# Moving the loads of the next head's keys, queries and values from the first unit of a head to behind its first two projection tasks

## The chip, the core and the metric

The kernel runs on one core of a Trainium2 chip. The metric is the device time of one execution in microseconds (us). TensorE (PE), VectorE (DVE), ScalarE (ACT), GpSimd (POOL) and SyncE (SP) each run their own list of instructions and meet through semaphores. SP computes nothing here: it issues transfers, one after the other, to 16 DMA engines that all queues share.

## The reference, cut to what matters

Two transformer-like layers follow one another. The part that this text is about is the first attention: 1024 latent tokens and 6404 context rows of width 128 are normalised, and 16 heads of width 64 are computed over 7428 keys (context and latents).

```python
q = lat @ Wq
kv = jnp.concatenate([x, lat], axis=1) @ Wkv
k, v = jnp.split(kv, 2, axis=-1)
dots = jnp.einsum('bhid,bhjd->bhij', q, k) * scale     # 16 heads, 1024 x 7428
attn = jax.nn.softmax(dots, axis=-1)
out = jnp.einsum('bhij,bhjd->bhid', attn, v)
```

After it come an output projection, a layer of experts, a second attention and a second layer of experts.

## The kernel before, in words

`stage_attention` works head by head. A head has 60 units (`UNITS`), numbered g = 0 to 59; a unit takes two tiles of 128 keys against half of the queries. In each unit PE makes scores (L583, L584), ACT takes the exponential (L725), POOL splits off the low half of the probabilities (L518) and PE multiplies high and low halves by the values (L599, L601, L611). Beside this, PE scores for the running maximum of the next head from unit 24 on (`OFFSET`, L559) with a reduction on DVE (L788).

Heads go in pairs: head b = 2i (the even head, e = 0) and head 2i + 1 (the odd head, e = 1). During a pair, every third unit has a task that projects a block for the next pair: in the even head 17 tasks for queries and keys, in the odd head 15 tasks for values. A task is a chain: PE projects into bank Y (L531 to L533 or L541 to L543), ACT copies the high half into a staging buffer (`copy_kq`, L689, or `copy_v`, L697), DVE writes the low half (L765, L773), SP writes both to device memory (L419 and L420, or L428). There are two staging buffers of each kind (`NR` = 2), so task n uses buffer n % 2, and ACT waits with the copy of task n until the write of task n - 2 has landed (semaphores `kq_out`, `v_out`). That wait stands in ACT's one list, in front of the exponentials of the units that follow.

At the start of head b, SP loads what head b + 1 needs into the other half of the double buffers: `load_kq` (six transfers, 3.2 MB: keys twice, low keys, queries) and, in an even head, also `load_v` (1.9 MB). The wait ahead of it is for the last score of head b - 1. The values of the next even head are loaded in unit 51 of the odd one.

PE, ACT and DVE run the pairs in a hardware loop of seven turns (`Fori(0, HEADS // 2 - 1)`), whose body is two heads; the last pair is straight code behind it. So there are six backward jumps, each at the start of an even head (b = 2, 4, ... 12). POOL has a loop of its own over one head. SP's list has no loop.

Of the kernel before, what the change touches and what calls it, by code (L numbers as in the profile page):

```python
# [26 lines left out]
HEADS, DH = 16, 64  # L27
# [286 lines left out]
def stage_attention(nc, pers, A):  # L314
# [5 lines left out]
    with sc:  # L320
# [48 lines left out]
        TASKS = KQ_TASKS + V_TASKS  # L369
        TASK_STEP = 3  # L370
        BACK_AT, FRONT_AT = 26, 56
        EARLY = 2 * (UNITS - OFFSET)
        FIRST_SLOTS = [[]] * 3 + [list(range(n, n + EARLY // 12)) for n in range(0, EARLY, EARLY // 12)]

# [6 lines left out]
        def task_at(e, g):  # L381

            n = g // TASK_STEP
            if g % TASK_STEP or n >= (V_TASKS if e else KQ_TASKS):
                return None
            return KQ_TASKS + n if e else n
# [19 lines left out]
        def _(sp):  # L406
# [3 lines left out]
            def write_kq(i, n, high, low, done):  # L410

                sp.wait_ge(y_split, i * TASKS + n + 1)
                r, w = slice(i * P, (i + 1) * P), twidth(n)
                if n < Q_TASKS:
                    oh, ol = (d[r, n * BANK:n * BANK + w] for d in (q_high, q_low))
                else:
                    c = (n - Q_TASKS) * BANK
                    oh, ol = (d[r, c:c + w] for d in (k_high, k_low))
                sp.dma_start(oh, high[:, 0:w]).then_inc(done, 16)  # L419
                sp.dma_start(ol, low[:, 0:w]).then_inc(done, 16)  # L420

            def write_v(i, n):
                sp.wait_ge(y_split, i * TASKS + n + 1)
                r, tt = (n - KQ_TASKS) % NR, vtiles(n)
                w = full_tiles(n)
                c = slice(tt[0] * VCOLS, (tt[0] + w) * VCOLS)
                o = v_all[2 * i * P:(2 * i + 2) * P, c].rearrange("(a p) c -> p a c", p=P)
                sp.dma_start(o, stage_v[r][:, :, 0:w, :].rearrange("p a t c -> p a (t c)")).then_inc(v_out[r], 16)  # L428
                if w < len(tt):
                    c = slice(FULL_TILES * VCOLS, KEY_TILES * VCOLS)  # L430
                    for a in range(2):
                        o = v_all[(2 * i + a) * P:(2 * i + a) * P + TAIL, c]
                        sp.dma_start(o, stage_v[r][0:TAIL, a, w, :]).then_inc(v_out[r], 16)

            def v_writes(i, r):

                tasks = [n for n in range(KQ_TASKS, TASKS) if (n - KQ_TASKS) % NR == r]
                return OUT0 + 16 * i * sum(1 if full_tiles(n) == len(vtiles(n)) else 3 for n in tasks)

            def kq_writes(i, r):  # L440
                return OUT0 + 32 * (i - 1) * len(range(r, KQ_TASKS, NR))

            def load_kq(m):
                e = m % 2
                sp.dma_start(kc[0:DH, e, :], k_high[rows(m), :]).then_inc(k_in[e], 16)
                sp.dma_start(kc[DH:P, e, :], k_high[rows(m), :]).then_inc(k_in[e], 16)
                sp.dma_start(qc[0:DH, e, :], q_high[rows(m), :]).then_inc(q_in[e], 16)
                sp.dma_start(qc[DH:P, e, :], q_low[rows(m), :]).then_inc(q_in[e], 16)
                sp.dma_start(qd[0:DH, e, :], q_high[rows(m), :]).then_inc(q_in[e], 16)
                sp.dma_start(kd[0:DH, e, :], k_low[rows(m), :]).then_inc(k_in[e], 16)  # L450

            def load_v(m):
                e, whole = m % 2, FULL_TILES * VCOLS
                sp.dma_start(v[:, e, 0:FULL_TILES, :].rearrange("p t c -> p (t c)"),
                             v_all[m * P:(m + 1) * P, 0:whole]).then_inc(v_in[e], 16)
                sp.dma_start(v[0:TAIL, e, FULL_TILES, :], v_all[m * P:m * P + TAIL, whole:KEY_TILES * VCOLS])\
                  .then_inc(v_in[e], 16)
# [12 lines left out]
            for b in range(HEADS):  # L470
                i, e = divmod(b, 2)
                projecting = i + 1 < HEADS // 2
                for g in range(UNITS):
                    if g == 0 and b + 1 < HEADS:
                        if b:
                            sp.wait_ge(scored, b * UNITS)
                        if b and e:
                            for r in range(NR):
                                sp.wait_ge(kq_out[r], kq_writes(i + 2, r))
                        load_kq(b + 1)  # L480
                        if not e:
                            if b:
                                sp.wait_ge(low_done, LOW0 + b * UNITS)
                            load_v(b + 1)
                    if projecting:
                        n = task_at(e, g)
                        if n is not None and n < KQ_TASKS:
                            r = n % NR
                            write_kq(i + 1, n, stage_h[r], stage_l[r], kq_out[r])
                        elif n is not None:  # L490
                            write_v(i + 1, n)
                        if e and g == LAST - 8:
                            for r in range(NR):
                                sp.wait_ge(v_out[r], v_writes(i + 2, r))
                            sp.wait_ge(low_done, LOW0 + b * UNITS)
                            load_v(b + 1)
# [264 lines left out]
        def _(dve):  # L761
# [43 lines left out]
            def head(b, e, with_max, projecting, i):  # L805
                for g in range(UNITS):
                    m, _, n = slots_at(b, e, g)
                    slots = with_max or m is b
                    if slots:
                        take(m, n)  # L810
                    t = task_at(e, g - 1) if projecting and g else None
                    if t is not None:
                        split_task(i + 1, t)
                    if slots:
                        take(m, n + 1)
                        if n + 2 in (SLOTS // 2, SLOTS):
                            finish_max(m, 0 if n + 2 < SLOTS else 1)
                    if g % SIDE == PAIRS:
                        normalize_half(b, g // SIDE)
# [734 lines left out]
def build(nc, a, out):  # L1554
    attention = dict(x=a["x"], ctx=a["ctx_1024"], ln_m_g=a["L0_xattn_ln_m_g"], ln_m_b=a["L0_xattn_ln_m_b"],
                     ln_l_g=a["L0_xattn_ln_l_g"], ln_l_b=a["L0_xattn_ln_l_b"], wq=a["L0_xattn_Wq"],
                     wkv=a["L0_xattn_Wkv"], wout=a["L0_xattn_Wout"])
    experts0 = dict(control=a["L0_ffn_controller"], up=a["L0_ffn_f1"], up_bias=a["L0_ffn_bias"], down=a["L0_ffn_f2"])
    cross = dict(ctx=a["ctx_1024"], w_cq=a["L1_xattn_w_cq"], b_cq=a["L1_xattn_b_cq"], w_c=a["L1_xattn_w_c"],
                 b_c=a["L1_xattn_b_c"], w_q=a["L1_xattn_w_q"], b_q=a["L1_xattn_b_q"], w_l=a["L1_xattn_W_l"],  # L1560
                 b_l=a["L1_xattn_b_l"])
    experts1 = dict(control=a["L1_ffn_Wc"], control_bias=a["L1_ffn_bc"], up=a["L1_ffn_W1"], up_bias=a["L1_ffn_b1"],
                    down=a["L1_ffn_W2"], down_bias=a["L1_ffn_b2"])
    whole = Scope(nc, "all")
    with whole:
        pers = Persistent(whole)
        shared = Scope(nc, "shared")
        with shared:
            for_attention(pers, shared)
            stage_prepare(nc, pers, attention)  # L1570
            stage_attention(nc, pers, attention)
            stage_attention_out(nc, pers, attention)
        whole.clear_semaphores()
        later = Scope(nc, "later", whole)
        with later:
            for_later_stages(pers, later)
            ahead = dict(ctx=cross["ctx"], up=experts1["up"], down=experts1["down"])
            stage_experts(nc, pers, experts0, "experts0", 0, ahead=ahead)
            stage_cross(nc, pers, cross)
            stage_experts(nc, pers, experts1, "experts1", 1, out)  # L1580
# [26 lines left out]
```

## Time and profile before

| what | value |
| --- | --- |
| median of three runs | 2737.18 us (2736.98 to 2744.89) |
| time of the profiled execution | 2738.75 us |
| its span, first to last instruction | 2737.0 us |
| PE busy / ACT / DVE / POOL | 92% / 49% / 62% / 67% |
| mean granted TensorE clock | 0.963 of full speed |
| data moved by the DMA engines | 172.13 MB |

The span is what the trace covers; the profiled execution's time is 1.75 us more than its span and 1.57 us above the median. Busy times are unions of an engine's instructions. A time at the start of a row of a timeline is in us from the span's start; in square brackets at its end stands how long the engine sat idle before it, and what released it. "issue" there means that no semaphore of the profile explains the wait. The granted clock of 1.00 is TensorE's upper level (2.4 GHz), 0.50 the lower (1.2 GHz).

### The profile page before, as it was taken

How to read it: one execution, taken by the hardware profiler on the slowest of the kernel's cores; microseconds unless marked ns; L12 is line 12 of the kernel's file. 1: busy time of each engine (PE TensorE's matmuls, PEld its weight loads, DVE VectorE, ACT ScalarE, POOL GpSimd, SP SyncE). 2: the span in 40 equal slices, each digit the busy share in tenths (PEclk: the TensorE clock that was granted, in tenths of full speed). 3: DMA queues.
4: the chain of work that ended last, by engine and by line, in shares of the span. 5: the costliest groups of instructions: out<-in, count | busy, mean ns of one | idle time of the engine just before them, and what ended most of it. 6: DMA issues, size and time to landing. Idle time of an engine off the chain costs nothing. (4 is left out here: it accounts for less than half of the span.)

```text
span 2737.0 us, 83713 instructions
## 1 busy us (share of the span) xinstructions
PE 2515.7 (92%) x33785; PEld 1679.6 (61%) x33785; DVE 1693.1 (62%) x3186; ACT 1343.9 (49%) x1627; POOL 1840.3 (67%) x1056
## 2 busy tenths in 40 slices
PE   3479998999899989998999899989999999769996
PEld 1236665666566656665666566656666666547884
DVE  8566665666566656665666566656666662248764
ACT  4125554555455545554555455545555555227652
POOL 1128887888788878887888778877888999501001
PEclk9779999999999999999999999999999999879998
DMA  2441314131413141213122321232132200150000
GB/s 83 142 137 40 75 41 120 40 75 42 119 43 76 41 119 41 67 48 100 60 59 60 91 69 52 64 83 77 39 80 69 56 2 2 59 127 1 2 2 11
DMA packets 98555, 172.13 MB, mean 63 GB/s; under 512 B 10280, under 2 KB 87664, under 8 KB 92656
## 3 DMA queue, kind: packets, MB, share of 16 engines
q1 hardware_dynamic: 94864, 162.46, 20.7%
q8 instruction: 285, 4.67, 0.8%
q10 hardware_dynamic: 3296, 4.10, 0.5%
q14 instruction: 110, 0.90, 0.1%
HBM read 100.72 MB, written 65.81 MB: 61 GB/s over the span
## 5 line engine op out<-in xcount | busy, mean ns | idle before, releaser
L518 POOL TENSOR_TENSOR att_prob_low<-att_prob 128x1024 f16<-128x1024 f32 x960 | 1787.8, 1864 | 488.4 <-ACT att_prob L725 407.0
L788 DVE TENSOR_REDUCE att_part<-all_banks 128x1 f32<-128x512 f32 (+1 forms) x1920 | 1242.1, 669 | 753.6 <-PE all_banks L559 736.9
L725 ACT ACTIVATE att_prob<-all_banks 128x1024 f32<-128x1024 f32 x960 | 968.8, 1009 | 874.4 <-PE all_banks L584 805.7
L559 PE MATMUL all_banks<-att_kc,att_qc 128*128 128x512 f16 (+1 forms) x1920 | 718.9, 379 | 96.0 <-issue 72.9
L583 PE MATMUL all_banks<-att_qc,att_kc 128*128 128x512 f16 (+1 forms) x1888 | 719.5, 381 | 0.7 <-issue 0.7
L584 PE MATMUL all_banks<-att_qd,att_kd 128*128 128x512 f16 (+1 forms) x1888 | 719.6, 381 | 0.0
L599 PEld LDWEIGHTS all_banks<-att_v,att_prob 128*128 128x128 bf16 x7552 | 537.9, 99 | 131.7 <-issue 15.5
L599 PE MATMUL all_banks<-att_v,att_prob 128*128 128x65 f16 x7552 | 594.3, 193 | 5.8 <-ACT att_prob L725 5.8
L601 PE MATMUL all_banks<-att_v,att_prob 128*128 128x64 f16 x7552 | 595.9, 194 | 0.5 <-issue 0.5
L601 PEld LDWEIGHTS all_banks<-att_v,att_prob 128*128 128x128 bf16 x7552 | 505.6, 97 | 100.3 <-issue 0.3
L611 PEld LDWEIGHTS all_banks<-att_v,att_prob_low 128*128 128x128 f16 x7552 | 351.0, 97 | 115.7 <-POOL att_prob_low L518 6.4
L611 PE MATMUL all_banks<-att_v,att_prob_low 128*128 128x65 f16 x7552 | 382.1, 193 | 5.8 <-POOL att_prob_low L518 2.9
L584 PEld LDWEIGHTS all_banks<-att_qd,att_kd 128*128 128x128 f16 (+1 forms) x1888 | 184.6, 98 | 211.9 <-issue 4.4
L559 PEld LDWEIGHTS all_banks<-att_kc,att_qc 128*128 128x128 f16 x1920 | 186.1, 98 | 141.6 <-issue 81.1
L583 PEld LDWEIGHTS all_banks<-att_qc,att_kc 128*128 128x128 f16 (+1 forms) x1888 | 184.7, 98 | 135.7 <-issue 10.5
L982 POOL MEMSET experts_tie<- 128x1 f32 x64 | 2.2, 98 | 225.4 <-POOLq L1177 195.6
L697 ACT ACTIVATE att_stage_v<-all_banks 128x512 f16<-128x512 f32 (+1 forms) x120 | 70.8, 591 | 148.5 <-PE all_banks L543 122.1
L689 ACT ACTIVATE att_stage_h<-all_banks 128x512 f16<-128x512 f32 (+1 forms) x119 | 69.6, 585 | 81.5 <-PE all_banks L533 74.0
L773 DVE TENSOR_TENSOR att_stage_v<-all_banks,att_stage_v 128x256 f16<-128x256 f32 (+1 forms) x240 | 87.2, 405 | 34.4 <-ACT att_stage_v L697 33.5
L1359 DVE TENSOR_TENSOR cross_pt_l<-all_banks,cross_pt_h 128x512 f16<-128x512 f32 (+1 forms) x112 | 70.8, 641 | 36.2 <-ACT cross_pt_h L1309 35.8
L541 PE MATMUL all_banks<-shared_wv_h,shared_kvh 128*128 (+2 forms) x472 | 89.3, 225 | 1.0 <-DVE att_prob L765 1.0
L543 PE MATMUL all_banks<-shared_wv_h,shared_kvl 128*128 (+2 forms) x472 | 89.6, 225 | 0.0
(272 smaller groups left out, 2066.3 us busy)
## 6 DMA issues: line engine op xcount, KB each, us to landing
att_v<-v_all SPq DMA_DIRECT2D x16, 1870.5 KB
att_kc<-k_high SPq DMA_DIRECT2D x32, 928.5 KB, 10.9
v_all<-att_stage_v SPq DMA_DIRECT2D x112, 258.0 KB, 2.5
att_kd<-k_low SPq DMA_DIRECT2D x16, 928.5 KB, 15.3
k_high<-att_stage_h SPq DMA_DIRECT2D x98, 128.0 KB, 1.7
k_low<-att_stage_l SPq DMA_DIRECT2D x98, 128.0 KB, 1.9
prep_ctx<-in_ctx SPq DMA_DIRECT2D x5, 640.0 KB, 10.4
later_ctx<-in_ctx SPq DMA_DIRECT2D x1, 3200.0 KB
```

The lines of the kernel that those rows point to most:

```text
L518: pool.tensor_tensor(prob_low[g % NL][0:n, 0:w], p[:, 0:w], p.bitcast(BF16)[:, 1:2 * w:2], op=ALU.subtract).then_inc(low_split, 1)
L541: pe.matmul(o, th, wh, start=True, stop=False)
L543: last = pe.matmul(o, tl, wh, start=False, stop=True)
L559: pe.matmul(X[n % 2][:, 0:kwidth(c)], qc[:, e, j * P:(j + 1) * P], kc[:, e, c * BANK:c * BANK + kwidth(c)], start=True, stop=True).then_in ...
L583: pe.matmul(o, kc[:, e, t * P:t * P + n], qc[:, e, q], start=True, stop=False)
L584: last = pe.matmul(o, kd[:, e, t * P:t * P + n], qd[:, e, q], start=False, stop=True)
L599: pe.matmul(O[:, o:o + DH + 1], w, v[:, e, t, 0:DH + 1], start=False, stop=False, skip_group_check=True)
L601: last = pe.matmul(O[:, o:o + DH], w, v[:, e, t, DH + 1:VCOLS], start=False, stop=False, skip_group_check=True)
L611: last = pe.matmul(O[:, o:o + DH + 1], w, v[:, e, t, 0:DH + 1], start=False, stop=True, skip_group_check=True)
L725: act.activation(o, i, ACT.Exp, scale=SCALE).then_inc(exp_done, 1)
L773: last = dve.tensor_tensor(st[:, a, 0:w, DH + 1:VCOLS], y, st[:, a, 0:w, 0:DH], op=ALU.subtract)
L788: dve.tensor_reduce(part[:, j, c:c + 1], X[n % 2][:, 0:kwidth(c)], axis=AX.X, op=ALU.max)\
```

## The change

The condition under which SP issues the loads in `block.sync` goes from unit 0 to unit 4. SP's list is written unit by unit, and tasks 0 and 1 of a head stand at units 0 and 3, so the loads now stand behind the writes of these two tasks and before the write of task 2.

```diff
         BACK_AT, FRONT_AT = 26, 56
+        LOAD_AT = 4
...
                 for g in range(UNITS):
-                    if g == 0 and b + 1 < HEADS:
+                    if g == LOAD_AT and b + 1 < HEADS:
                         if b:
                             sp.wait_ge(scored, b * UNITS)
                         if b and e:
                             for r in range(NR):
                                 sp.wait_ge(kq_out[r], kq_writes(i + 2, r))
                         load_kq(b + 1)
                         if not e:
                             if b:
                                 sp.wait_ge(low_done, LOW0 + b * UNITS)
                             load_v(b + 1)
```

SP's list at the start of an even head, before. The names h0, l0, h1 and l1 are the two staging buffers of high and low halves; kc, kd, qc, qd and v are the loaded operands:

```order
L445 DMA att_kc<-k_high 64x7428
L446 DMA att_kc<-k_high 64x7428
L447 DMA att_qc<-q_high 64x1024
L448 DMA att_qc<-q_low 64x1024
L449 DMA att_qd<-q_high 64x1024
L450 DMA att_kd<-k_low 64x7428
L454 DMA att_v<-v_all 128x7482
L456 DMA att_v<-v_all 4x129
L419 DMA q_high<-att_stage_h0 128x512
L420 DMA q_low<-att_stage_l0 128x512
L419 DMA q_high<-att_stage_h1 128x512
L420 DMA q_low<-att_stage_l1 128x512
```

The same place on SP with the change (all line numbers are one higher), from the write of task 1 on:

```order
L420 DMA q_high<-att_stage_h1 128x512
L421 DMA q_low<-att_stage_l1 128x512
L446 DMA att_kc<-k_high 64x7428
L447 DMA att_kc<-k_high 64x7428
L448 DMA att_qc<-q_high 64x1024
L449 DMA att_qc<-q_low 64x1024
L450 DMA att_qd<-q_high 64x1024
L451 DMA att_kd<-k_low 64x7428
L455 DMA att_v<-v_all 128x7482
L457 DMA att_v<-v_all 4x129
L420 DMA k_high<-att_stage_h0 128x512
L421 DMA k_low<-att_stage_l0 128x512
```

The eight loads have moved from ahead of the write of task 0 to between the writes of tasks 1 and 2. In an odd head SP's list before is the loads and then the writes of values:

```order
L449 DMA att_qd<-q_high 64x1024
L450 DMA att_kd<-k_low 64x7428
L428 DMA v_all<-att_stage_v0 128x2x516
L428 DMA v_all<-att_stage_v1 128x2x516
L428 DMA v_all<-att_stage_v0 128x2x516
```

and with the change:

```order
L429 DMA v_all<-att_stage_v1 128x2x516
L446 DMA att_kc<-k_high 64x7428
L447 DMA att_kc<-k_high 64x7428
L448 DMA att_qc<-q_high 64x1024
L449 DMA att_qc<-q_low 64x1024
L450 DMA att_qd<-q_high 64x1024
L451 DMA att_kd<-k_low 64x7428
L429 DMA v_all<-att_stage_v0 128x2x516
```

Here six loads have moved behind two writes. In head 14 no tasks stand in the list, and its loads stay where they were. The lists of PE, ACT, DVE and POOL are the same before and after.

## Rows read from the trace of the kernel before

**Rows 1.** Who waited for whom: us in total, times, longest

```profile
PE all_banks L559 <- issue: 72.9, 7, 22.1
```

**Rows 2.** Windows, an even and an odd head: busy us, instructions, clock, DMA

```profile
448.50:592.80 144.30, 135.36 (x1845) 85.76 (x1845) 88.26 (x144) 71.68 (x79) 111.87 (x61) 0.96 0.24 68
592.80:725.60 132.80, 132.79 (x1971) 90.03 (x1972) 87.93 (x158) 70.75 (x79) 111.84 (x61) 1.00 0.25 70
```

**Rows 3.** Timeline of PE at the first jump, and at the sixth

```profile
452.28 0.53 PE L611 MATMUL all_banks<-att_v,att_prob_low 128*128 128x65 f16 x12
461.75 0.61 PE L559 MATMUL all_banks<-att_kc,att_qc 128*128 128x512 f16 x1 [8.94 <-issue]
...
1848.68 0.61 PE L559 MATMUL all_banks<-att_kc,att_qc 128*128 128x512 f16 x1 [8.92 <-issue]
```

**Rows 4.** DMA queues: packets, MB, share; 451.3:457.7, then 457.7:459.5

```profile
q1 hardware_dynamic: 107, 1.35, 101.7%
...
q8 instruction: 1, 0.02, 4.7%
q14 instruction: 2, 0.02, 4.5%
```

**Rows 5.** Instruction packets: 306.0:307.0, 314.4:315.4, none until 328.8:329.8

```profile
q8 instruction: 1, 0.02, 6.2%
...
q8 instruction: 1, 0.02, 6.0%
...
q8 instruction: 1, 0.02, 8.6%
```

**Rows 6.** Windows at the first jump, behind the sixth, and behind 201.28

```profile
452.80:455.10 2.30, 0.01 (x1) 0.00 (x0) 0.61 (x2) 0.00 (x0) 1.03 (x1) 0.99 1.00 213
...
461.75:465.30 3.55, 3.55 (x9) 1.41 (x10) 1.38 (x2) 0.60 (x1) 1.45 (x1) 0.50 0.97 203
...
1848.68:1854.53 5.85, 5.85 (x43) 3.38 (x44) 1.38 (x2) 1.62 (x2) 2.08 (x2) 0.50 0.99 237
201.28:205.89 4.61, 4.61 (x47) 3.17 (x48) 1.44 (x3) 1.59 (x2) 3.79 (x2) 0.50 0.16 57
```

**Rows 7.** Timeline of SP, ACT and PE in head 0

```profile
182.80 0.43 SPq L420 DMA_DIRECT2D q_low<-att_stage_l  x1
...
199.72 0.60 ACT L689 ACTIVATE att_stage_h<-all_banks 128x512 f16<-128x512 f32 x1 [7.46 <-DMA q_low<-att_stage_l]
...
201.28 0.24 PE L599 MATMUL all_banks<-att_v,att_prob 128*128 128x65 f16 x1 [5.37 <-ACT att_prob L725]
```

**Rows 8.** Timeline of SP in head 2: loads, second write, third write

```profile
448.54 0.45 SPq L445 DMA_DIRECT2D att_kc<-k_high  x1
...
474.68 0.32 SPq L419 DMA_DIRECT2D q_high<-att_stage_h  x1
475.05 0.43 SPq L420 DMA_DIRECT2D q_low<-att_stage_l  x1
481.44 0.32 SPq L419 DMA_DIRECT2D k_high<-att_stage_h  x1
```

**Rows 9.** Timeline of ACT in head 2, copy of task 4

```profile
491.73 0.60 ACT L689 ACTIVATE att_stage_h<-all_banks 128x512 f16<-128x512 f32 x1 [0.58 <-PE all_banks L533]
```

**Rows 10.** DMA issues, us to landing: from 467.9, from 330.3

```profile
q_low<-att_stage_l SPq DMA_DIRECT2D x1, 128.0 KB, 5.5
...
v_all<-att_stage_v SPq DMA_DIRECT2D x1, 258.0 KB, 4.0
```

**Rows 11.** Timeline of head 1: SP's loads and writes, ACT's fifth copy

```profile
315.00 0.45 SPq L445 DMA_DIRECT2D att_kc<-k_high  x1
...
323.61 28.13 SPq L428 DMA_DIRECT2D v_all<-att_stage_v  x5
...
348.36 0.61 ACT L697 ACTIVATE att_stage_v<-all_banks 128x512 f16<-128x512 f32 x1 [0.76 <-PE all_banks L543]
```

**Rows 12.** Timeline of PE in head 1

```profile
331.76 0.20 PE L611 MATMUL all_banks<-att_v,att_prob_low 128*128 128x65 f16 x1 [0.53 <-issue]
```

## The prediction, made before the changed kernel had run

> **What bounds the kernel now.** I read the windows of whole heads first. An odd head keeps PE busy for 132.79 of 132.80 us; an even head behind a jump takes 144.30 us with PE busy for 135.36 [rows 2]. So PE bounds both, every us in which PE stands adds to the time, and even heads have some 9 us of standing that odd ones lack. The list of waits names it: PE waited seven times before L559 for nothing that a semaphore explains, 72.9 us in all, the longest 22.1 us [rows 1]. That longest one lies ahead of the first head, at 104 us. The other six are (72.9 - 22.1) / 6 = 8.47 us each, and the timeline puts them at the six backward jumps: 8.94 us at the first, 8.92 at the last [rows 3]. PE had ended at 452.81 (452.28 + 0.53) and went on at 461.75.
>
> What PE waits for is its own code. After SP issued the loads from 448.54 on, no packet of an instruction queue (q8, q14) is seen from 451.3 to 457.7, while the load's queue q1 alone fills the DMA engines (101.7%); then q8 and two of q14 come together, and work goes on behind them [rows 4]. That the loads make code late also shows where nothing jumps. In running code q8 brings a packet about every 8.3 us (one in 306.0:307.0, one in 314.4:315.4), but under the loads of head 1 the next comes only in 328.8:329.8, about 14.3 us after the last, 6.0 us late [rows 5], and PE starves for 0.53 us [rows 12].
>
> The stop has a second price. Behind it TensorE runs at a granted clock of 0.50 (1.2 GHz), having stood idle before: 3.55 us behind the first jump, 5.85 behind the sixth [rows 6], on average 4.46 over the six. At half speed that loses half of it, 2.2 us. A jump so costs 8.47 + 2.2 = 10.7 us.
>
> **Part 1: the jump without the loads.** The changed SP list puts the loads behind the write of task 1, some 13 us after PE goes on, so the jump's code meets empty DMA queues. The trace has no such jump. Lower bound of the gain: the code is no less than 4.9 us late, since PE stopped at 452.81 and no code packet came before 457.7 [rows 3, 4], and if a shorter stop still lowers the clock nothing else is gained: about 5.0 us per jump. Upper bound: code comes 6.3 us earlier and the clock stays up, 8.5 us. I take 5.8 us, a little under the 6.0 of running code [rows 5], which leaves PE idle for about 2.7 us, and I take it that such a stop leaves the clock at its upper level, since after PE's end at 452.81 the records still show 0.99 until 455.1 [rows 6]. That is 5.8 + 2.2 = 8.0 us per jump, **-48 us** over six.
>
> **Part 2: even heads, a write behind the loads.** The moved item is eight transfers in a queue that serves in order. What is late next is the write of task 2, which is now issued behind them and which frees staging buffer 0 for the copy of task 4. Before, it was the write of task 0 that stood behind the loads, and the jump's standstill hid that.
>
> Head 0 has no jump and shows the stall undisguised. The low write issued at 182.80, behind the loads, held ACT's copy until 199.72, idle 7.46 us; PE then stood for 5.37 us [rows 7]. A copy that nothing holds follows an idle time of 0.58 us [rows 9]. So the copy was 7.46 - 0.58 = 6.9 us late, and PE has a slack of 6.9 - 5.37 = 1.5 us. Behind it the clock was low for 4.61 us [rows 6], 2.3 us lost: 7.7 us in all.
>
> Now the same for a head with the change, by the distances of head 2. The write of task 1 ends its issue at 475.05 + 0.43, about 475.5 [rows 8]: call this L, the moment of the first load. The write of task 2 is issued at 481.44, L + 6 [rows 8]. The copy of task 4 starts at 491.73, L + 16.2 [rows 9]. When does the write land? Before, the low write issued at 468.30 took 5.5 us, so it landed at 473.8, 25.3 us after the first load at 448.54 [rows 8, 10]; a free write of this size takes about 2 us, so the queue of loads held it. I take 25 us. The copy is 25 - 16.2 = 8.8 us late, PE stands 8.8 - 1.5 = 7.3 us, and with 2.3 us of low clock the head pays 9.6 us. Ends: 7.6 if the write lands after 23 us because PE's stop is gone, 10.4 at 25.3 us with a longer low clock. Six heads: **+58 us**. Head 0 already pays 7.7, so it adds **+1.9 us**.
>
> **Part 3: odd heads.** The loads are six transfers here. SP issues them at 315.00 [rows 11]; the write of values from 330.3 on landed 4.0 us later, at 334.4 [rows 10], 19.4 after the first load. With the change the first load stands behind that write, at 330.8. The write of the third task is then behind the loads and lands at 330.8 + 19.4 = 350.2. The fifth copy starts at 348.36 [rows 11]: 1.8 us late, 1.5 of it in the slack, 0.3 us on PE. Seven heads: **+2.4 us**, between 0 and 7.
>
> **What costs nothing.** The loads land later, but the first reader is the maximum of unit 24, and they end some 25 us after unit 5, near unit 17; the values are read in the next head. SP's wait in front of the loads is for a score long past. In head 14 nothing moves. Code packets in the shifted loads come late while PE runs: one starvation like [rows 12] in each of 14 heads would be 7 us, but some heads had it already; I take 0 and keep 5 for the range.
>
> **The sum.** 2738.75 (the profiled execution, 1.57 us over the median) - 48 + 58 + 1.9 + 2.4 = 2753 us; less 1.57 this is 2751 us against the median. A big gain and a big loss all but cancel. The turning point: with the jump at -8.0, the change pays only if the stall of an even head is under about 7.3 us.
>
> **Rivals.**
> - *The code is late for another reason, and the jump stays as it is.* Then part 1 is 0: 2737 + 58 + 1.9 + 2.4 = 2799 us. For it: a taken jump needs new code whatever else runs, and no jump here is seen without loads. Against it: the packet that is 6.0 us late in head 1, where nothing jumps [rows 5]. The Trainium skill speaks for this rival ("DMA: Bandwidth & Descriptors", section on queues, rings and completion order): a DMA engine takes turns between the queues it has work for, packet by packet, so that a code packet would wait for little more than one packet of the loads. By that rule the loads could not make the jump long and the time would be the 2799 us above; by the row it is 2751. The trace disagrees with the rule so far.
> - *Writes are not held by the loads* (the faster side). If the write of task 2, issued only 6 us behind the first load, slips through by L + 17.7, the stall of even heads is gone: 2737 - 48 - 7.7 (head 0's too) + 0 = 2682 us; half of it gone leaves about 2715. It decides at L + 23: later than that the change loses. Against it: head 0's writes, issued at 182.80, did not land before 199 [rows 7].
> - *Even balance.* The loads end a little sooner (23.3 us), the stall costs 7.9 us, and all of it comes to within 8 us of 2737.
>
> **How the numbers follow.** What a measurement here can tell from no change is about 0.3%, 8.2 us. Main case with a stall of 8 to 10.4 us: 0.60; even balance: 0.20; jump stays: 0.09; writes slip through or stall under 7 us: 0.11. Slower by over 0.3%: 0.60 and 0.09, less some of the main case's low end: 0.66. Within: 0.22. Faster: 0.12. The main case's own range: -51 to -30 from part 1, +45 to +62 from even heads, 0 to +12 from the rest, that is 2731 to 2781. The 80% range leaves out most of the two far cases: 2729 to 2783.
>
> **What the profile will show.** Right: PE's idle before L559 at the six jumps is 2 to 4 us instead of 8.5; the low clock behind jumps is gone; and in seven even heads ACT's L689 waits some 9 us for a write of k_low, PE some 7 us for L725, about 30 us into the head, with low clock behind. Wrong if the jumps still cost 8 us (first rival), if L689 waits for no DMA (second), or if PE stands at the jump for under 1 us. Odd heads should be within 1 us of 133.

## The result, and the profile after

The changed kernel takes 2761.01 us (median of 6 runs, 2758.62 to 2763.37) against 2737.14 us before. The medians lie 23.9 us apart; the ratio estimated from all runs is 1.0078, with a 95% interval from 1.0067 to 1.0090, which is 21 us (18 to 25). The changed kernel is slower. The prediction had 2751 us, in 2729 to 2783, and slower as the likeliest case. The span of the profiled execution is 2756.8 us, 19.8 more than before.

First the waits of the changed kernel that answer to [rows 1] and [rows 7] (us in total, times, longest):

```profile
ACT att_stage_h L690 <- DMA k_low<-att_stage_l: 62.3, 7, 9.2
PE all_banks L600 <- ACT att_prob L726: 59.2, 16, 7.1
ACT att_stage_v L698 <- DMA v_all<-att_stage_v: 53.0, 8, 23.3
PE all_banks L560 <- issue: 35.8, 7, 21.8
```

The last row is the one in which the jumps stand. Without the one long wait ahead of head 0, (35.8 - 21.8) / 6 = 2.33 us are left per jump, where it was 8.47. The first row is new: in seven even heads ACT's copy waits for a write of low keys. The second is what that does to PE: 59.2 us of standing in front of L600, of which before there were 5.4 us in head 0 and crumbs. The third row holds a wait of 23.3 us before the loop, as before, and seven new ones of 3.7 to 5.1 us in odd heads.

The timeline of PE in head 2, at the jump and at the new stop, against [rows 3]:

```profile
455.50 0.39 PE L560 MATMUL all_banks<-att_kc,att_qc 128*128 128x512 f16 x1 [2.10 <-issue]
...
493.67 0.23 PE L600 MATMUL all_banks<-att_v,att_prob 128*128 128x65 f16 x1 [6.83 <-ACT att_prob L726]
```

and SP and ACT between the two, against [rows 8] and [rows 9]:

```profile
466.72 0.32 SPq L420 DMA_DIRECT2D q_high<-att_stage_h  x1
467.08 0.43 SPq L421 DMA_DIRECT2D q_low<-att_stage_l  x1
467.56 0.47 SPq L446 DMA_DIRECT2D att_kc<-k_high  x1
...
473.84 0.43 SPq L421 DMA_DIRECT2D k_low<-att_stage_l  x1
...
492.10 0.60 ACT L690 ACTIVATE att_stage_h<-all_banks 128x512 f16<-128x512 f32 x1 [8.91 <-DMA k_low<-att_stage_l]
```

The loads start at 467.56. The low write of task 2 is issued at 473.84, 6.3 us behind them, and the copy that waits for it starts at 492.10, 24.5 us behind the first load. Its idle time of 8.91 less the usual 0.58 is 8.3 us of lateness; PE stands for 6.83.

The windows (same columns as [rows 2]) show what each head pays, and where the clock is low:

```profile
452.00:596.90 144.90, 135.97 (x1842) 86.40 (x1841) 88.38 (x144) 71.52 (x80) 111.97 (x60) 0.98 0.24 68
596.90:732.20 135.30, 133.07 (x1968) 89.92 (x1967) 88.05 (x158) 70.56 (x79) 111.83 (x60) 1.00 0.24 69
455.50:459.00 3.50, 3.50 (x45) 2.25 (x46) 1.39 (x3) 1.62 (x2) 2.08 (x2) 1.00 0.03 7
737.40:740.80 3.40, 3.40 (x39) 2.45 (x38) 0.99 (x2) 1.34 (x2) 0.97 (x2) 0.50 0.01 2
493.70:498.40 4.70, 4.70 (x46) 3.05 (x47) 1.71 (x3) 1.47 (x2) 3.78 (x2) 0.50 0.18 61
```

The even head is as long as before (144.9 against 144.3 us): it stands for 144.90 - 135.97 = 8.93 us, now 2.10 at the jump and 6.83 at the late copy. The odd head (head 3) takes 135.3 us and stands for 2.23 us, where it stood for 0.01; I had said within 1 us of 133. Behind the first jump the clock stays at 1.00. Behind the second it is at 0.50 for 3.4 us, and behind the late copy for 4.7 us.

### The profile page after: what moved, and what is told of

Read it like the earlier page. It is cut to its first block and busy times, and to the rows that moved or that the text cites. A ratio compares the mean times of both kernels' runs of the same rounds, so it can differ in the third digit from the quotient of the medians.

```text
span 2756.8 us, 83713 instructions
## 1 busy us (share of the span) xinstructions
PE 2519.1 (91%) x33785; PEld 1680.3 (61%) x33785; DVE 1694.9 (61%) x3186; ACT 1342.1 (49%) x1627; POOL 1841.5 (67%) x1056
## 5 line engine op out<-in xcount | busy, mean ns | idle before, releaser
L560 PE MATMUL all_banks<-att_kc,att_qc 128*128 128x512 f16 (+1 forms) x1920 | 720.3, 379 | 58.7 <-issue 35.8
L600 PEld LDWEIGHTS all_banks<-att_v,att_prob 128*128 128x128 bf16 x7552 | 540.2, 99 | 190.0 <-ACT att_prob L726 73.7
L600 PE MATMUL all_banks<-att_v,att_prob 128*128 128x65 f16 x7552 | 597.6, 193 | 59.3 <-ACT att_prob L726 59.2
L766 DVE TENSOR_TENSOR att_stage_l<-all_banks,att_stage_h 128x512 f16<-128x512 f32 (+1 forms) x119 | 79.3, 666 | 45.3 <-ACT att_stage_h L690 45.3
L1360 DVE TENSOR_TENSOR cross_pt_l<-all_banks,cross_pt_h 128x512 f16<-128x512 f32 (+1 forms) x112 | 70.9, 642 | 36.3 <-ACT cross_pt_h L1310 35.8
```

The source lines that it names most:

```text
L560: pe.matmul(X[n % 2][:, 0:kwidth(c)], qc[:, e, j * P:(j + 1) * P], kc[:, e, c * BANK:c * BANK + kwidth(c)], start=True, stop=True).then_in ...
L600: pe.matmul(O[:, o:o + DH + 1], w, v[:, e, t, 0:DH + 1], start=False, stop=False, skip_group_check=True)
L766: dve.tensor_tensor(low[:, 0:w], src[:, 0:w], high[:, 0:w], op=ALU.subtract).then_inc(y_split, 1)
```

## The experiments

Each ratio is against the kernel before, run beside it on the same chip. The kernel before had medians from 2738.93 to 2739.65 us there.

**Even heads alone, and odd heads alone.** The two runs split the change.

```diff
-                    if g == LOAD_AT and b + 1 < HEADS:
+                    if g == (0 if e else LOAD_AT) and b + 1 < HEADS:     # e1; e2: (LOAD_AT if e else 0)
```

> The loads move behind tasks 0 and 1 in even heads alone; in odd heads they stay at unit 0. My theory (jump freed, one write held behind the loads): PE idle at the six jumps about 2.3 us, ACT's L689-copy of task 4 idle some 9 us in seven even heads, no copy of values waits for a DMA. The even heads of the changed kernel were 8.4 us longer in sum than before, head 0 0.3 shorter, so about +8 us: 2745. Rival (the odd heads' loss comes from the even heads' change, by loads that drain later or code that comes late): the odd heads stay long by 14 us, and the time is near 2760.

> The loads move in odd heads alone; in even heads they stay at unit 0, so the jumps stay at 8.5 us idle. My theory: the seven odd heads lose what they lost in the changed kernel, 14 us, all of it by the copy of the fifth values task waiting for the write behind the loads: 2751. Rival (odd heads lose because the even head before them changed): no change, 2737.

Measured: e1 2753.2 us, ratio 1.0047 (1.0035 to 1.0059), and e2 2749.53 us, ratio 1.0041 (1.0027 to 1.0054). The two excesses add up to 0.88%, the change itself has 0.78%. The waits of e1:

```profile
ACT att_stage_h L690 <- DMA k_low<-att_stage_l: 63.1, 7, 10.0
PE all_banks L560 <- issue: 35.5, 7, 21.5
ACT att_stage_v L698 <- DMA v_all<-att_stage_v: 24.7, 4, 22.9
```

and of e2:

```profile
PE all_banks L560 <- issue: 71.8, 7, 21.5
ACT att_stage_v L698 <- DMA v_all<-att_stage_v: 51.3, 8, 23.1
ACT att_stage_h L690 <- DMA q_low<-att_stage_l: 8.5, 1, 8.5
```

In e1 the short jumps and the seven late copies of keys come together, and of the odd heads' waits for values 1.8 us in three are left (24.7 - 22.9). In e2 the jumps are long again ((71.8 - 21.5) / 6 = 8.4 us), and the seven waits for values are there. Each loss belongs to its own kind of head, so the rival of both runs falls. e1 came out 14 us above the kernel before, 6 more than I had expected from the even heads of the changed kernel. In its trace the clock accounts for that. It was low behind all six short jumps, as here behind the first (columns as in [rows 2]):

```profile
456.72:459.89 3.17, 3.17 (x8) 1.25 (x9) 1.38 (x2) 0.60 (x1) 1.59 (x1) 0.50 0.03 8
```

The changed kernel had it low behind two of the six. That is 13 us more at the lower level, 6.5 us lost.

**A third staging buffer.** If the write held behind the loads is the cause, a buffer that is needed one task later takes it away and leaves the loads where they are.

```diff
-        NR = 2
+        NR = 3
...
-            sp.wait_ge(filled, 4)
+            sp.wait_ge(filled, NR + 2)
```

> The changed kernel with three staging buffers of each kind instead of two, so that a copy waits for the write three tasks back. The held copy of an even head comes 6.75 us later, which takes its lateness from about 8.3 to 1.6 us, within the slack of 1.5 to 2 us; in odd heads it is gone. My theory: jumps 2.3 us idle with the clock up (-48 to -52 us), head 0's old stall gone (-8), no new stall: 2678 to 2690. Rival (the stops in even heads come from the loads themselves, beside running PE, and not from the wait for the write): the stops of 7 us stay and the time is near 2750.

Measured: 2689.92 us, ratio 0.9819 (0.9795 to 0.9842), 49 us faster than before and some 70 us faster than the change with two buffers. Its waits:

```profile
PE all_banks L560 <- issue: 35.6, 7, 21.9
ACT att_stage_h L690 <- DMA k_low<-att_stage_l: 15.3, 7, 2.6
PE all_banks L600 <- ACT att_prob L726: 2.0, 6, 0.7
```

The copies still wait, but 2.2 us each (15.3 / 7), 1.6 late, and of 59.2 us of standing on PE 2.0 are left. The loads run beside PE exactly as in the changed kernel, so they are not what stopped it.

**The control: a third buffer without the change.** The same edit on the kernel before.

> Control for the third staging buffer: the kernel before, loads at unit 0, with three buffers of each kind. My theory: only head 0's stop (5.4 us and 2.3 us of low clock) goes, the jumps stay at 8.5 us: about 2730. Rival (the third buffer alone is what gained the 49 us): 2690.

Measured: 2730.95 us, ratio 0.9963 (0.9949 to 0.9977).

```profile
PE all_banks L559 <- issue: 74.1, 7, 21.7
ACT att_stage_h L689 <- DMA q_low<-att_stage_l: 1.7, 1, 1.7
```

The jumps stay at (74.1 - 21.7) / 6 = 8.7 us, and only head 0's stop goes. The buffer alone gives 9 us. The other 40 us of e3 come from moving the loads, once nothing waits behind them.

**Half the dose.** The changed kernel, but the values of an even head are loaded from unit 28.

```diff
+        LOAD_AT, LOAD_V_AT = 4, 28
...
                         load_kq(b + 1)
-                        if not e:
-                            if b:
-                                sp.wait_ge(low_done, LOW0 + b * UNITS)
-                            load_v(b + 1)
+                    if g == LOAD_V_AT and not e:
+                        if b:
+                            sp.wait_ge(low_done, LOW0 + b * UNITS)
+                        load_v(b + 1)
```

> The changed kernel, two buffers, with one thing less behind task 1 of an even head: the values are loaded from unit 28, keys and queries stay at unit 4. The write of task 2 then stands behind six transfers instead of eight. My theory: it lands some 20 us after the first load instead of 25, the copy of task 4 is 3 to 4 us late as in odd heads (3.0 to 4.4), PE stands 1 to 2.5 us instead of 7 in seven even heads and the clock mostly stays up: 6 to 8 us less per even head than the changed kernel, 2705 to 2720, with odd heads as in the changed kernel. Rival (the stop is a fixed price of a write behind any load): 7 us stays, 2760.

Measured: 2708.88 us, ratio 0.9885 (0.9869 to 0.9902).

```profile
ACT att_stage_h L690 <- DMA k_low<-att_stage_l: 22.9, 7, 3.7
PE all_banks L600 <- ACT att_prob L726: 19.0, 16, 2.4
```

With 3.2 MB instead of 5.0 ahead of the write, the copy is idle 3.3 us instead of 8.9, and all stops on PE, of both kinds of head, fall from 59.2 to 19.0 us. The stop grows with what stands ahead of the write; it is no fixed price. In its trace the clock was low behind five of the six short jumps.

**Another place.** `LOAD_AT = 10`: the loads stand behind the writes of tasks 0 to 3.

> The changed kernel with LOAD_AT = 10: the loads stand behind the writes of tasks 0 to 3. My theory: the held write is now that of task 4 and the late copy that of task 6, by the same distances, so nothing is gained or lost against the changed kernel: six jumps at 2.3 us, seven stops of 7 us in even heads, seven of 1 to 3 us in odd ones, 2761 within 5 us. Rival (the place right behind the jump is what makes the stop long, by cold clock or by code fetches that follow the jump): stops well under 7 us, under 2745.

Measured: 2757.28 us, ratio 1.0068 (1.0047 to 1.0089), the same as the change within the intervals.

```profile
ACT att_stage_h L690 <- DMA k_low<-att_stage_l: 65.7, 7, 9.9
PE all_banks L600 <- ACT att_prob L726: 52.9, 11, 7.8
```

In head 2 the late copy is now that of task 6, at 509.29 instead of 492.10, and at least as late (9.94 us idle). The stop moves with the loads: while they stay in one piece, this later place costs the same. Other places were not tried.

**Spread loads.** The version that the above points to, with two buffers: never more than one large transfer of keys between two writes, and the values later.

```diff
+        LOADS_AT, LOAD_V_AT = (4, 7, 10), 28
...
+                    if g in LOADS_AT and b + 1 < HEADS:
+                        load_part(b + 1, LOADS_AT.index(g))     # one of kc, kc, kd, with one of the query loads
+                    if g == LOAD_V_AT and not e:
+                        if b:
+                            sp.wait_ge(low_done, LOW0 + b * UNITS)
+                        load_v(b + 1)
```

> The changed kernel with two staging buffers, but the loads in four portions: one transfer of high keys and one of queries behind the write of task 1, the same again behind task 2, low keys and queries behind task 3, and in even heads the values from unit 28. No write stands behind more than 1.1 MB of keys or 1.9 MB of values, 5 to 9 us of transfers, and the copy needs it only 16 us after. My theory: jumps 2.3 us idle, no copy waits for a DMA: 2680 to 2690. Rival (any load beside running PE costs some us per head, by late code): ten or more stops of 0.5 us before PE without a releaser, and 2695 or more.

Measured: 2687.09 us, ratio 0.9801 (0.9777 to 0.9824). This is the lowest time of the study, but its interval overlaps that of e3.

```profile
ACT att_stage_v L707 <- DMA v_all<-att_stage_v: 23.9, 1, 23.9
PE all_banks L569 <- issue: 14.4, 6, 2.8
```

No copy inside the loop waits for a transfer; the wait of 23.9 us is the one ahead of it. The jumps have 14.4 / 6 = 2.4 us each. The rival's stops of 0.5 us by late code did not come: inside the loop PE has no idle time of over 0.4 us except at the jumps.

**How loads make code late: small packets, and few bytes.** Two runs on the other half of the change. e5 is the kernel before, with every load of keys and values cut into four pieces:

```diff
-                sp.dma_start(kc[0:DH, e, :], k_high[rows(m), :]).then_inc(k_in[e], 16)
+                for c in range(0, KEYS, PIECE):        # PIECE = KEYS // 4; kd likewise, the values in pieces of 15 tiles
+                    sp.dma_start(kc[0:DH, e, c:c + PIECE], k_high[rows(m), c:c + PIECE]).then_inc(k_in[e], 16)
```

> The kernel before, loads at unit 0, but each row of keys (14.9 KB) is loaded in four transfers of a quarter row and the values in four of about 3.9 KB per row: the same bytes in packets of a quarter of the size. The question is how the loads make the jump's code late. If a code packet stands behind a fixed number of packets that the DMA engines already hold (some five of 1.2 us each make the 6 us seen), it now waits for about 1.5 us: PE idle at the jumps 3 to 4 us, clock mostly up, about 2700. If it stands behind the bytes, or behind whatever was issued ahead of it, the jumps stay at 8 us idle and the time at 2737. If the jump is long by itself, also 2737, but that the changed kernel's 2.1 to 2.5 us already speak against.

Measured: 2709.3 us, ratio 0.9895 (0.9878 to 0.9911). PE and DVE at the first jump:

```profile
PE all_banks L564 <- issue: 44.8, 7, 20.8
...
455.83 0.60 PE L564 MATMUL all_banks<-att_kc,att_qc 128*128 128x512 f16 x1 [4.03 <-issue]
...
460.27 1.29 DVE L793 TENSOR_REDUCE att_part<-all_banks 128x1 f32<-128x512 f32 x2 [7.68 <-issue]
```

PE stands for (44.8 - 20.8) / 6 = 4.0 us, half of before. The clock was low behind all six jumps, not mostly up as I had expected. Code does come sooner: between 450 and 456 us this trace has three code packets,

```profile
q8 instruction: 1, 0.02, 1.4%
q14 instruction: 2, 0.02, 1.3%
```

where the kernel before had none until 457.7. That the number came as expected does not prove the reason, because the cut changed two things. The packets are a quarter as large, but SP had also put fewer bytes into the queue when PE stopped: seven pieces of 0.23 MB (1.6 MB), where before it was six transfers (3.2 MB). And DVE does not fit. Its last instruction before the jump ends at 452.59, 0.8 us after PE's, and it stands for 7.68 us. Until 456.43 it also lacked the scores of PE's first matmul, but for the other 3.8 us it lacked its code. Had code stood behind a fixed number of small packets, it should have been there by then. SP was still issuing pieces (until 461.6) when DVE asked; whether that is why DVE's code came late is not shown.

e8 tests the amount: spread loads with large packets, but the first transfer of high keys, 0.93 MB, is back at unit 0, ahead of the jump, and the first query load is at unit 13.

```diff
-        LOADS_AT, LOAD_V_AT = (4, 7, 10), 28
+        LOADS_AT, LOAD_V_AT = (0, 7, 10, 13), 28
```

> Spread loads, but the first transfer of high keys (0.93 MB) is back at unit 0, in front of the jump, and all else behind tasks 2, 3 and 4 (values from unit 28). Theory A (a code packet waits for what was put into the DMA queues before it was asked for, up to some 6 to 7 us): the transfer of 0.93 MB drains in about 7 us, code comes 2 to 4 us late, PE stands 4 to 6 us at the jumps; 2695 to 2712. Theory B (any large load in flight delays code by the full 6 us): 8.5 us idle at the jumps, 2730. Theory C (only a deep queue of several transfers does): 2.3 us, 2687.

Measured: 2706.76 us, ratio 0.9877 (0.9859 to 0.9894).

```profile
PE all_banks L570 <- issue: 27.2, 6, 4.8
```

27.2 / 6 = 4.5 us per jump: between the 2.4 us of no load and the 8.5 of the full load, as theory A has it. With packets of one size, code waits longer the more has been put in ahead of it. (The rest of the 20 us between e8 and e4 is clock: low for 26.5 us behind the jumps, against 13.6.) Bytes alone do not order all runs, though: e5 had 1.6 MB ahead of the jump and stood for 4.0 us, e8 0.93 MB and 4.5 us. So the size of the packets seems to count as well.

## Why the prediction was right, and where it was off

The mechanism was right: the jumps got short, and a write held behind the loads cost about as much again; the runs showed both halves apart. Two sizes were off, that of the odd heads and that of the clock behind short jumps. The sizes, read from the trace of the changed kernel, a us of low clock counted as half a us lost:

| term | predicted | measured |
| --- | --- | --- |
| six jumps | -48 | -36.8 of idle time, -10.0 of low clock: -46.8 |
| stops in six even heads | +58 | 41.3 idle + 14.1: +55.4 |
| head 0 | +1.9 | +0.7 |
| seven odd heads | +2.4 | 11.0 idle + 1.4: +12.4 |

The sum is +21.7 us, where the prediction's was +14.3; the spans differ by 19.8, the ratio says 21.

**Jumps.** The idle time went from 8.47 to 2.33 us; I had said 2.7. That TensorE keeps its upper level behind so short a stop held at four of six; behind the jumps at 736 and 1021 it was low for 3.4 us each. It is less sure than that: in the traces of the six kernels with short jumps (the changed one, e1, e3, e4, e7 and e9), the lower level followed 22 of 36. With the clock of e1 the term would be about -40 (-36.8 of idle time, -3.4 of low clock), so its nearness to -48 is in part luck. The rival in which the jump stays as it is has fallen, since the jumps got short once no load was in front of them. The Trainium skill ("DMA: Bandwidth & Descriptors", section on queues, rings and completion order), whose rule I had set beside that rival, counts typically 9 to 17 descriptors as one packet. I had read its packet as one of the profile, which here is one row of 14.9 KB. The first code packet came 4.9 us after PE's stop, too late for a wait of one such row (about 1.2 us); how many rows make up a packet of that page no run here shows, so the rule is neither borne out nor refuted. e1 has the short jumps with odd heads untouched, e2 the long ones.

**Even heads.** The copy started 24.5 us after the first load, released by the write (25 assumed), the copy was 8.3 us late (8.8), PE stood for 6.83 (7.3). Head 0, which had shown the stall before the change, was a good model: the slack of 1.5 us carried over to 0.1 us. e3, with e6 as its control, and e7 show that the wait for the write is the cause.

**Odd heads: the term that was mis-sized.** The step that was off is the lateness of the fifth copy: 1.8 us, with 1.5 of it in the slack. The stops on PE were 0.87 to 2.68 us instead of 0.3. Two readings were off. First, 348.36 was taken for the time of an unhindered copy, but in that head the loads had already delayed PE: the code starvation of [rows 12], 0.53 us, stands ahead of it, and copies that are elsewhere 6.7 us apart were 7.6 apart there. In the changed kernel the copy would have come 16.6 us after the first load, not 17.5; it came at 19.6 and was 3.0 us late (the stop was 0.87 us, so the slack there is about 2 us and not 1.5). Second, I used one head for seven. In head 5, say, the idle time before the copy is 5.09 us:

```profile
892.82 1.74 SPq L446 DMA_DIRECT2D att_kc<-k_high  x1
...
913.87 0.60 ACT L698 ACTIVATE att_stage_v<-all_banks 128x512 f16<-128x512 f32 x1 [5.09 <-DMA v_all<-att_stage_v]
```

The copy starts 21.05 us after the first load there. The write of task 1 is issued only 0.48 us before the loads and is under way when they start, and the first load lands after 9.0 to 9.2 us in heads 1 and 5, where it took 7.1 in head 1 before. That the write in front delays them would fit, but no run here took it away alone.

**What stays open.** Why code is late by up to 6 or 7 us and not more, though the loads take over 20 us to drain, isn't settled. A fixed number of packets does not fit DVE in e5, and the waiting grows with what was issued (e8). Whether the limit is one of bytes or of time no run told apart. Why the clock fell behind some short jumps and not behind others is open too. And no run issued the writes from another engine, so whether SP's queue holds them or the DMA engines that they share with the loads is not told apart. Strictly in order they do not land: in head 2 of the changed kernel the high write of task 3, issued at 480.12, landed after 11.1 us, at 491.2, and the low write of task 2, issued at 473.84, after 18.2 us, at 492.0.

## What to carry to other kernels

A loop's jump needs its code at once, over the same DMA engines that loads fill: keep large loads out of the few us ahead of it. A load that is moved takes its place in one queue with small writes, and a write that frees a buffer is then as late as everything ahead of it. So ask of each move which write now stands behind the load and when its buffer is wanted; spread the load between the writes, or add a buffer. If the trace has one undisguised example of the stall, as head 0 here, model the new stalls on it; but take the unhindered time from a place where nothing is late yet.

## What the runs showed of the hardware

A backward jump with no load in flight cost PE 2.1 to 2.8 us of idle time (changed kernel and spread loads), 4.3 to 4.8 us with 0.93 MB ahead of it (e8), and 7.9 to 8.9 us with the full load (kernel before). Cutting the rows of the load into quarters took 4.5 us off PE's idle time at a jump (e5), but at the first jump DVE still lacked its code 3.8 us after PE's scores were there.

A stop of 2.1 to 2.8 us at a jump was followed by the lower clock level in 22 of 36 cases; the stops of 3.0 us and more at the jumps of the kernel before, e5 and e8 were followed by it in all 18, and those of 5.4 us and more in front of L600 in the changed kernel and the one before in all 8.

A write of 128 KB took 1.9 us to land with nothing ahead of it ([rows 8], the low write behind the one at 481.44) and 18.2 us when it was issued 6.3 us behind the first of 5.0 MB of loads (the low write at 473.84 in the changed kernel).
